# Pair 0 of a blended feed-forward kernel: two products on each weight block, an earlier DRAM trip, and reordered queues

## What is computed

```python
h = gelu(embedding @ W0 + b0); h = gelu(h @ W1 + b1)
att = softmax(h @ W2 + b2)
agg_w = einsum('bk,koi->boi', att, weight[..., 0]); agg_b = att @ bias_k
y = einsum('boi,bih->boh', agg_w, x) + agg_b[:, :, None]
out = y @ W.T + b
scores = y @ gate_w.T + gate_b          # 4 ranks: 8, 16, 32, 64
lora = y @ A[:r].T @ B[:, :r].T         # r is the rank with the top score
result = x + out + lora
```

## Time and profile before

| | us |
|---|---|
| median of 3 runs | 458.93 (458.45 to 459.08) |
| the profiled execution's own time | 458.18 |
| its span in the trace | 456.3 |
| PE busy | 450.4 |
| DVE busy | 343.8 |
| ACT busy | 181.4 |

### The profile page before, as it was taken

How to read it: one execution, slowest core, us unless ns; L and a number is a source line. 1 busy time by engine, 2 the same in 40 slices (tenths; PEclk the granted TensorE clock), 3 DMA queues, 4 the chain that set the end, 5 groups by cost and what they waited for, 6 DMA issues and landing times.

```text
span 456.3 us, 10477 instructions
## 1 busy us (share of the span) xinstructions
PE 450.4 (99%) x3510; PEld 445.8 (98%) x3510; DVE 343.8 (75%) x889; ACT 181.4 (40%) x415; POOL 19.4 (4%) x46
## 2 busy tenths in 40 slices
PE   9999999899999999999999999999999999999997
PEld 7999999899999999999999999999999999999997
DVE  4887988799586876958687695868769586876945
ACT  5654554455243343524334342433334243342511
POOL 1010000010000000000000000000000000100000
PEclk9999999999999999999999999999999999999999
DMA  7973560711608053250805235080523408052202
GB/s 273 344 277 54 145 227 1 239 46 52 232 1 278 6 188 97 88 195 0 281 1 194 88 90 192 0 278 4 201 81 108 174 5 277 0 190 95 92 2 93
DMA packets 23773, 59.18 MB, mean 130 GB/s; under 512 B 6862, under 2 KB 8834, under 8 KB 23684
## 3 DMA queue, kind: packets, MB, share of 16 engines
q1 hardware_dynamic: 23508, 58.78, 39.0%
q10 hardware_dynamic: 240, 0.07, 0.1%
HBM read 40.69 MB, written 18.15 MB: 129 GB/s over the span
## 4 chain that ended last, share of the span: by engine, by line
PE 96%; DVE 3%; ACT 1%; issue 0%; POOL 0%; ACTq 0%; POOLq 0%
PE p_p L1071 74%; PE p_o L1089 4%; PE p_o L1091 4%; PE p_o L1109 3%; PE p_o L1090 3%; PE p_o L1108 3%; PE p_p L1115 1%; PE p_p L1136 1%; PE p_p L1097 1%; PE p_o L1136 1%; DVE wl L716 1%; DVE w_raw L722 1%; DVE zl L792 0%; DVE aggw L776 0%; DVE prod L773 0%
## 5 line engine op out<-in xcount | busy, mean ns | idle before, releaser
L1071 PE MATMUL p_p<-wh,xh 128*128 128x274 f32 (+1 forms) x880 | 256.6, 292 | 0.0
L1071 PE MATMUL p_p<-wh,xl 128*128 128x274 f32 (+1 forms) x880 | 254.2, 289 | 0.0
L1071 PE MATMUL p_p<-wl,xh 128*128 128x272 f32 (+1 forms) x864 | 250.5, 290 | 0.0
L1071 PEld LDWEIGHTS p_p<-wh,xh 128*128 128x128 f32 x880 | 166.5, 189 | 0.4 <-issue 0.4
L1071 PEld LDWEIGHTS p_p<-wh,xl 128*128 128x128 f32 x880 | 166.7, 189 | 0.1
L1071 PEld LDWEIGHTS p_p<-wl,xh 128*128 128x128 f32 x864 | 163.0, 189 | 0.1
L579 ACT ACTIVATE zh<-sv 128x274 fp32r<-128x274 f32 (+1 forms) x56 | 24.3, 433 | 95.0 <-DVE sv L804 95.0
L811 DVE TENSOR_TENSOR xin<-p_o,xin 128x274 f32<-128x274 f32 (+2 forms) x128 | 52.0, 418 | 2.7 <-PE p_o L1109 1.9
L557 ACT ACTIVATE xh<-s_raw 128x512 fp32r<-128x512 f32 x60 | 36.3, 628 | 17.1 <-DVE s_raw L759 16.4
L579 ACT ACTIVATE zh<-p_p 128x272 fp32r<-128x272 f32 (+1 forms) x44 | 17.5, 398 | 60.7 <-PE p_p L1071 59.0
L766 DVE TENSOR_TENSOR xl<-s_raw,xh 128x512 fp32r<-128x512 f32 x60 | 40.9, 682 | 0.1
(11 more groups left out here) (140 smaller groups left out, 508.4 us busy)
## 6 DMA issues: line engine op xcount, KB each, us to landing
xin<-in_x SPq DMA_DIRECT2D x32, 512.0 KB, 4.0
raw<-in_xt SPq DMA_DIRECT2D x31, 512.0 KB, 5.2
out<-xin SPq DMA_DIRECT2D x30, 512.0 KB, 5.9
w_raw<-in_w SPq DMA_DIRECT2D x8, 274.0 KB, 7.0
w_raw<-in_w SPq DMA_DIRECT2D x8, 272.0 KB, 6.0
g_aggw<-aggw_all SPq DMA_DIRECT2D x8, 128.0 KB, 2.4
aggw<-g_aggw SPq DMA_DIRECT2D x15, 64.0 KB, 5.0
out<-xin SPq DMA_DIRECT2D x4, 137.0 KB, 2.1
```

What stands on the lines that cost most here:

```text
L1071: last = nc.tensor.matmul(o[:, 0:W[r]], a, m, start=start and p == 0, stop=stop and p == 2, skip_group_check=True)
```

## The change

1. **Order of blocks.** Round 0's blocks are now loaded in the order B12, B22, B11, B21 (`W_ORDER`, `FIRST_W`, the host's `blocks`). PE takes both products on a block when it comes: B12 for Z12 and Z22, B22 for Z12 and Z22, then B11 and B21 for Z11 and Z21. The order in which Z's are finished is a table, `MADE`; buffers and waits follow it (`made`, `z_place`). The banks of the first two column sums change places.
2. **keep_busy** inside the first block is gone (two times two matmuls).
3. **x of pair 0** comes in smaller pieces: A11's rest, A21, A12, A22, each with a semaphore or place of its own.
4. **The kernel rows' trip.** `kern_s` is loaded earlier, `kern_h` is made by ACT in place of DVE, `kern_l` earlier on DVE; SP stores both and fetches `k_rows` ahead of the loads of x for the residual (`xin`) and of the next pair's x.
5. **Queues in pair 0.** DVE and ACT follow the new order; `attention_rows` stands behind the third unit, `attention_products` in the middle of the fifth.
6. **Pair 2.** One `t_sum` moves ahead of the second `bd_lo`, and `z_lo(Z11)` ahead of a `residual` and of the second `t_sum`.
7. **The end.** The last mix issues its two `zh` matmuls and the two of `lora` before it waits for `zl`.

```diff
-        W_ORDER = [(r, n, h) for r in range(2) for n in (B11, B21, B12, B22) for h in range(2)]
+        W_ORDER = [(r, n, h) for r, blocks in enumerate(((B12, B22, B11, B21), (B11, B21, B12, B22)))
+                   for n in blocks for h in range(2)]
...
-            first_unit(0, 0, 0)
+            first_unit(0, 2, 0, 0)
             pe.wait_ge(s_al, 2)
-            first_unit(0, 0, 1)
+            other_unit(0, 1, 0)
+            pe.wait_ge(s_al, 3)
+            first_unit(0, 2, 1, 1)
             attention_rows()
-            pe.wait_ge(s_al, 3)
-            first_unit(0, 1, 0, attention_products)
             pe.wait_ge(s_al, 4)
-            first_unit(0, 1, 1)
-            other_unit(0, 2, 0)
-            other_unit(0, 2, 1)
+            other_unit(0, 1, 1)
+            first_unit(0, 0, 0, 2, attention_products)
             other_unit(0, 3, 0)
-            mix(0, 0, 0, Z11)
-            other_unit(0, 3, 1)
-            pe.wait_ge(s_cs_lo, 2)
-            mix(0, 0, 0, Z22)
+            first_unit(0, 0, 1, 3)
             pe.wait_ge(s_aggbt, 2)
             pe.wait_ge(s_aggb, 1)
             mix(0, 0, 0, Z12)
-            first_unit(1, 0, 0)
-            first_unit(1, 0, 1)
+            pe.wait_ge(s_cs_lo, 1)
+            mix(0, 0, 0, Z22)
+            other_unit(0, 3, 1)
+            mix(0, 0, 0, Z11)
+            first_unit(1, 0, 0, 4)
+            first_unit(1, 0, 1, 5)
+            pe.wait_ge(s_cs_lo, 2)
             mix(0, 0, 0, Z21)
...
-                        if at < 2:
-                            keep_busy(2)
```

In the queues of ACT and SP the core of it is:

```diff
             w_hi(1)
+            act.wait_ge(s_raw_a21_in, 16)
+            nc.scalar.activation(a21h[:, :], raw[:, 1, 0:HB], ACT.Copy).then_inc(s_x1h, 1)
...
+            act.wait_ge(s_kern_s_in, 16)
+            nc.scalar.activation(kern_h[:, :], kern_s[:, :], ACT.Copy).then_inc(s_kern_hl, 1)
+            z_hi(0, 0, 0, Z12)
+            w_hi(6)
+            w_hi(7)
+            z_hi(0, 0, 0, Z22)
             cs_hi(0)
```

More of the change, by code:

```diff
@@ L37 @@
 P1, P6, P2, P5, P7, P3, P4 = range(1, 8)
+MADE = {Z12: 1, Z22: 2, Z11: 3, Z21: 4}
 SU2, SV, S22, S12, S21 = range(1, 6)
@@ L321, in piece, with made, z_place @@
             return count(i, j, PIECES, 4 * r + n)
+        def made(i, j, r, n):
+            return piece(i, j, r, MADE[n] if is_pair(i, j, 0) and r == 0 else n)
+        def z_place(i, j, r, n):
+            return (made(0, 0, 0, n) if is_pair(i, j, 0) and r == 0 else n) % 2 ^ 1
         def a_count(i, j, n):
@@ L370, in _ @@
                 sp.dma_start(bt_raw[half, :], bt).then_inc(s_lora_in, 16)
-            sp.wait_ge(s_al, 4)
-            for t in range(2):
-                sp.dma_start(raw[:, t, :], xt[2 + t]).then_inc(s_raw_in[t], 16)
+            sp.wait_ge(s_kern_hl, 2)
+            for n, rows in enumerate((kern_h, kern_l)):
+                sp.dma_start(g_kern[n].rearrange("k (a n) -> (k a) n", n=KC), rows[:, :].bitcast(F32)).then_inc(s_k_stored, 16)
             sp.wait_ge(s_aggbt, 1)
@@ L816, in route @@
                 dve.wait_ge(s_ubias, count(i, j, 1, 1))
-                dve.wait_ge(s_mix, piece(i, j, 0, Z12))
+                dve.wait_ge(s_mix, max(made(0, 0, 0, n) for n in (Z22, Z12)) if is_pair(i, j, 0) else piece(i, j, 0, Z12))
                 nc.vector.tensor_tensor(u[:, :, :], p_o[:, 1:3, U0:W[0]], ubias[:, :, :], ALU.add).then_inc(s_chain, 1)
@@ L980, in step @@
                     s_lo(i, j, S1)
+                if two:
+                    t_sum(0, R11, R12, R11)
                 bd_lo(i, j, 1)
+                if two:
+                    z_lo(i, j, 0, Z11)
                 if not one:
@@ L984, in step @@
                 if two:
-                    t_sum(0, R11, R12, R11)
                     t_sum(0, R12, R22, R12)
@@ L988, in step @@
                     s_lo(i, j, S3)
-                z_lo(i, j, 0, Z11)
+                if not two:
+                    z_lo(i, j, 0, Z11)
                 if one:
@@ L1081, in mix @@
             def mix(i, j, r, n):
-                t, at = TILE[n], (n - 1) % 2
-                pe.wait_ge(s_zl, piece(i, j, r, n))
-                if r == 0 and n in (Z11, Z22):
+                t, at = TILE[n], z_place(i, j, r, n)
+                pe.wait_ge(s_zl, made(i, j, r, n))
+                if r == 0 and n in ((Z12, Z22) if is_pair(i, j, 0) else (Z11, Z22)):
                     pe.wait_ge(s_bdl, count(i, j, 2, t + 1))
@@ L1354, with blocks @@
     low = (half + 3) // 4 * 2
-    def blocks(cols):
-        parts = [wag[k:k + kh, :, c + cols.start:c + cols.stop] for c in (0, half) for k in (0, kh)]
+    def blocks(cols, halves):
+        parts = [wag[k:k + kh, :, c + cols.start:c + cols.stop] for c in halves for k in (0, kh)]
         return np.stack([np.reshape(w, (2, kh // 2, P, -1)).transpose(0, 2, 1, 3) for w in parts])
@@ L1369 @@
         "bias_k": layer["bias_k"],
-        "w0": blocks(slice(low, half)),
-        "w1": blocks(slice(0, low)),
+        "w0": blocks(slice(low, half), (half, 0)),
+        "w1": blocks(slice(0, low), (0, half)),
         "b": ffn["b"],
```

170 lines of the change are left out of this document (93 added, 77 removed).

## The result

The changed kernel takes **456.52 us** (median of 6 runs, 455.94 to 457.63) against 458.69 for the kernel before beside it (6 runs, 458.40 to 459.20): ratio 0.9953, 95% interval 0.9939 to 0.9967. It is 2.2 us faster. The forecast was 457.4, 1.55 us faster, so the direction and the range held, and 0.65 us more came than the sum had. A second measurement gave 456.24 (9 runs) beside 458.66 (32 runs). The 0.65 us are at the edge of what these runs can tell: 0.9967, the upper end of the interval, is 1.5 us. The second measurement says the same as the first, and much of what follows is about them, because the runs point to the one edit that the prediction priced at nothing.

A forecast was written before the change was run, and what follows sets the result against it. PE, busy 99% of the span, was taken as the bound, so about 1% could move. Start +0.45, pair 2 -1.5 and end -0.5 sum to -1.55: median 458.93 becomes 457.4, own bounds 456.8 to 458.0, 8 in 10 456.0 to 458.6.

The forecast's parts named there:

- Point 1: First units of pair 0: without the filler matmuls PE is 0.91 us earlier, if its pace still rises at 9.6.
- Point 2: Pair 0's new order: DVE's chain from `attp` decides, round 1's first matmul at 29.06, 0.45 us later; range 0 to +0.5.
- Point 3: Kernel rows' DRAM trip: no wait of PE for `k_rows` in the trace, nothing to gain or lose, 0.
- Point 4: Round 1 of pair 0: DVE keeps its distance to PE, as all is moved by the same 0.45; 0.
- Point 5: Pair 2: `z_lo` done before PE needs it, so the wait at Z11's mix goes: -1.5 us, bounds 0 and -1.5.
- Point 6: Last five matmuls: four that don't need the low part fill the wait for it, -0.5 us.
- A: Pair 0's start gives what PE's work says, DVE's chain ending before PE comes: -1.8 there, 455.1 us; chance 10%.
- B: Pair 2's stall comes back later, at Z22 or a block sum: 458.9 us, no change; chance 12%.
- C: Slower: without fillers PE's pace rises later, each us costing 0.5; 459.9 us at 5 us and more; chance 5%.
- D: The start costs 1 us more, by a late x or ACT's list: 458.4 us; chance 8%.

The follow-up runs named there:

- Pair 2 alone: The kernel before with only pair 2's queue as changed: 457.12 us, ratio 0.9972.
- the trip alone: The kernel before with only the kernel rows' DRAM trip moved: 457.77 us, ratio 0.9966.
- the changed kernel's second time: The changed kernel run again without any edit, as the measure for other runs: 456.24 us, ratio 0.9945.
- start and trip: The changed kernel without the edits to pair 2 and to the end: 458.14 us, ratio 0.9972.
- products early: The changed kernel with attention_rows in the middle of the third unit and attention_products in the middle of the fourth: 455.30 us, ratio 0.9925.
- the end alone: The kernel before with only the last piece's five matmuls in the new order: 458.49 us, ratio 0.9993.

## Why the prediction was right, and where it was not

**Point 1, the fillers.** It said 0.91 earlier for PE, "if the pace still rises at 9.6". The pace rose at 4.3 in the profiled execution, and the second unit began at 9.91, 0.8 before the predicted 10.7. The condition was the weak part: the rise came anywhere between 4.3 and 10.0. "With no gap" did not hold either: at the faster pace PE waits in the first unit, which takes 3.50 us where 20 x 0.126 are 2.52, and with the fillers back it takes no longer. So at this pace the fillers stood in waits, and the 0.91 is not shown; at the slow pace, in the kernel before without them, `attp` came 0.64 earlier.

**Point 2, DVE's chain.** The mechanism is as told: 2.11 us of idle time ahead of `attp` (2.1 predicted), three waits at the mixes of Z12, Z22 and Z11. Round 1 began at 27.95 and not at 29.06, and this is no better chain but the earlier pace: `attp` came at 18.13 and not 18.91 (0.78), and the chain took 9.29 and not 9.56 (0.27). The predicted **+0.45** must be compared at the same pace. Pair 2 alone has the old start at an early pace (4.8): 27.55. The changed kernel (4.3) has 27.95: +0.40. A second pair says less: 28.13 for the trip alone (5.7) and 28.20 for the changed kernel's second time (5.9), +0.07; in the trip alone ACT stood 0.91 for the landing of b and DVE 1.92 for ACT's column sum. The medians say the same as the first pair (start and trip is 0.53 below before, the trip alone 0.89, so the start would cost 0.36), but the two kernels' executions overlap widely. That DVE's chain decides is shown by "products early"; that the start costs something is likely, and its size, 0.1 to 0.4, is open.

**Point 3, the trip. This is the step that failed:** "no wait of PE for it is in the trace. Nothing to gain." Two things were overlooked. The trace of before is one execution, with a late pace; by the estimate above `k_rows` landed 0.3 to 0.6 us before PE came, and the SP row could have said so: eight loads issued from 33.00 to 35.82 for a product at 42.47. At the same late pace another execution (the end alone) waits 0.35. And point 2 itself moves `attp`, with it the gate rows' stores, with them everything behind them on SP. With the trip left in place, the change would have been 2.1 us slower than before. Priced alone, the trip is -0.9 by the medians; that covers the 0.65 that the sum missed, and a little more.

**Point 4.** No wait in pair 0's round 1: right, thanks to point 3.

**Point 5, pair 2: -1.5.** Right, mechanism and size. The distance from round 1's first matmul to Z11's mix is 84.28 - 27.95 = 56.33, predicted 56.3; `z_lo` started at 82.76 after a wait of 0.39 for ACT, predicted until 83.4; and pair 2 alone measures -1.55.

**Point 6, the end: -0.5.** PE and DVE gain it: the five matmuls start 0.51 apart from first to last (450.09 to 450.60). The sum took it to the end of the kernel without asking what the last store does. It lands in 1.9 to 2.2 and not 1.7 (that the closer store ahead of it is the reason fits the rows, but no run changed it alone), and from the start of the last low part to the end of the span 0.2 us are left of it. The term was mis-sized: 0.5 predicted, 0.2 measured.

With the parts as measured alone, trip -0.9, start +0.35, pair 2 -1.55, end -0.2, the sum is -2.3, beside -2.2 and -2.4 measured. The close fit is partly luck: each of the first three terms is uncertain by some tenths. The prediction's own total also had some luck: it missed 0.9 at the trip, and the 0.3 too much that it gave to the end made up for a part.

**The rivals.** A (the start gives what PE's work says) did not come about in the change; "products early" shows that much of it was there to be had: round 1 begins 1.5 before the changed kernel's, and 1.1 before that of the old start at a like pace (26.48 against 27.55). B did not come. C neither: the pace rises early or late whether the fillers are there or not. D's cause, A21 landing late, is real: the prediction had it at about 8; where ACT waited for it, it came at 8.1 to 8.7 in five profiles and at 9.8 in one, and PE waited 0.52 and 1.25 us in two.

## What to carry to other kernels

A wait that is not in the trace of one execution is no proof of slack: compare when the last transfer of a chain is issued with when its reader comes, and ask what happens if the reader is 1 us earlier. When a step is moved later, follow all that stands behind it in the DMA queue, since there the cost can be larger than on the engine that is being watched. A long stall on TensorE can cost more than its length: in the one profile here that has it, 3.3 us of idle time cost 6.0, as the clock fell in it and came back only later. And an engine's gain at the very end counts only if the last store lands as much earlier.

## What was not expected of the hardware

- The moment at which PE's matmuls go from 0.227 to 0.126 us apart lay between 4.3 and 10.0 us in fourteen profiles, with the same instructions ahead of it in kernels at both ends. The granted-clock column stood at 1.00 throughout in the profile of before. From 9.6 to 4.8 us with the same start, round 1 came 1.06 us earlier (28.61 and 27.55).
- After 3.3 us without a matmul the granted clock was 0.53 over the next 6.5 us, though PE was busy for 6.44 of them; after the waits of 1.61 and 1.76 us in other profiles the matmuls kept their 0.127.
- With the two last stores of 137 KB issued 0.58 us apart, the last took 1.9 to 2.2 us to land (eight profiles); issued 1.07 us apart, 1.7 (six profiles).
- Stores of 16 KB with four loads of 512 KB issued right behind them took 7.9 to 10.3 us to land (five profiles). With two such loads behind them it was 4.8 to 7.2 in the changed kernel's two profiles, but up to 10.2 in "products early", so what sets it is not shown.
